# Round one of a graph-attention kernel: turns in pairs behind every second block, VectorE's edge codes one block later

## The chip, the cores and the metric

The kernel runs on one core of one Trainium2 chip. The metric is the time of one execution on the device, in microseconds. Three runs of the kernel before took 787.05 (the median), 786.87 and 788.37 us.

## The reference, cut to what matters

A layer norm, a graph attention layer over 4096 nodes with a dense 4096 x 4096 adjacency matrix, then a second layer (a state-space block). Only the attention touches the change:

```python
e = leaky_relu(feat_1 + feat_2.T, 0.2)       # rank one, before the nonlinearity
U = softmax(where(adj > 0, e, NEG_INF), axis=1)
prop_u = (0.5 * U) @ x                       # first product with U
rowsum = sum(U * (0.5 * U), axis=1)
feat = soft_threshold(f(x, prop_u, rowsum))
pu = U @ feat                                # second product with U
```

## The kernel before, in words

**The idea.** exp(leaky_relu(f1 + f2)) is exp(f1) exp(f2) where the sum is positive and exp(0.2 f1) exp(0.2 f2) where it is not. So each edge needs only one of three codes (no edge, edge with a negative sum, edge with a positive sum), and each product with U is two products with masks of ones and zeros: mask A times columns weighted one way, mask C times columns weighted the other way, scaled per row afterwards.

**Tiles and blocks.** The 4096 rows are 32 row tiles of 128. Four row tiles (`IT = 4`) are a supertile, so there are 8 supertiles. Round one is the first product with U, round two the second; round two also carries the state-space block, which is pipelined over its 32 row tiles. A row tile has 32 column tiles, taken in 4 blocks of 8 (`NB = 4`, `JB = 8`). A supertile has 16 blocks (`BLOCKS`), round one 128. Block b of a supertile works on row tile b // 4 and on column tiles 8 (b % 4) to 8 (b % 4) + 7.

**Two streams share each block of round one.** While the products of supertile G run, the codes of supertile G + 1 are made, two column tiles (`JH = 2`) for all four row tiles per block:
- SyncE loads half a megabyte of adj per block into one of four buffers (L344). The load of block h waits for the sign of block h - 4. At blocks 5, 8, 11 and 14 it also writes a row tile of the previous supertile's codes to HBM (L350), once all codes of that supertile are made; round two reads them back.
- ScalarE turns adj into bytes that say edge or no edge (`sign`, L1275).
- TensorE turns them to have columns on partitions: `turn`, four matmuls of 128 columns in bf16 with a unit matrix (L1640), into one of four PSUM banks. It waits for the sign and for the codes of four blocks back, whose bank it takes.
- VectorE compares and makes the codes (`codes`, L777), two instructions per block, which wait for the turn (`tr_done`).

**The products.** For block b ScalarE makes mask A (L1338) and VectorE mask C (L785) from the codes, two blocks ahead (`LEAD = 2`) and into one of four slots each; both wait until the product of four blocks before has ended, and for the codes. The masks of the first three blocks of a supertile need only part of the supertile's codes, those from the fourth block on need all of them (`mask1`: `NT if it else (ch + 1) * JB`, which is 32 for the fourth block as well). TensorE multiplies in two halves: 8 matmuls of 128 x 260 with mask A into accA (L1701) and 8 with mask C into accC (L1710), in float32 read in reduced form. It then turns. Before the first block of a row tile it waits until the accumulators of two row tiles ago were read (`free_acc`).

**Behind a row tile.** ScalarE reads accA in the second block of the next row tile (L1361, L1362). VectorE adds accC in the third (`sum1`, L802). GpSimd makes the tile's features out of the sum, a chain of some twenty small dependent instructions (`features`, L527 to L550). VectorE thresholds them one row tile later (`feat1`, L811 and L812), directly behind the next tile's sum.

**The order on each engine is written out by hand.** On VectorE a block of round one is: mask C for two blocks ahead, the two codes of this block, and in every fourth block a sum and a threshold. On TensorE: products, turn. On ScalarE: sign, mask A for two blocks ahead, in every fourth block a read of accA. In the last supertile there is nothing to turn; instead ScalarE (L1333), VectorE (L764) and, for three tiles, GpSimd prepare the weighted columns of round two, for which the features must be done. The line numbers in the rows are those of the kernel before.

## Time and profile before

| | |
|---|---|
| median of three runs | 787.05 us |
| the profiled execution, its own time | 786.87 us |
| its span, first to last instruction | 785.1 us |
| TensorE busy (matmuls) | 741.4 us, 94% |
| VectorE busy | 726.4 us, 93% |
| ScalarE busy | 671.1 us, 85% |
| GpSimd busy | 632.7 us, 81% |
| granted TensorE clock, mean | 0.991 of full speed |
| start of round one's steady part | 59.65 us (block 2) |
| last turn | 305.06 us |
| round two's products begin | 338.25 us |

The table gives the sums for the whole span. Engines run side by side, so the sums say nothing of which one sets the end; the order in time and the waits do. In the rows below an instruction's duration can reach over the start of the next one, because an engine takes up the next instruction before the last has drained; the step from start to start is then what one costs. Matmuls are pipelined, so theirs too are read from start to start.

### The profile page before, as it was taken

The numbers are of one execution on the slowest core, as the hardware profiler recorded it, in microseconds if no ns is written. First come the engines' busy times: TensorE is split into PE (matmuls) and PEld (weight loads), VectorE is DVE, ScalarE is ACT, GpSimd is POOL, SyncE is SP. The second block draws the span as 40 slices with busy tenths as digits, with TensorE's granted clock in tenths as the row PEclk, the third lists the DMA queues.
The fourth block names the chain that finished last, engine by engine and source line by source line (L and its number), as shares of the span: only waits on it lengthen the run. The fifth ranks groups of instructions, "written<-read, shape, count | busy, mean of one in ns | idle before, by whom it ended". The sixth has DMA issues, their size and how long they took to land.

```text
span 785.1 us, 21076 instructions
## 1 busy us (share of the span) xinstructions
PE 741.4 (94%) x6049; PEld 708.5 (90%) x6049; DVE 726.4 (93%) x1898; ACT 671.1 (85%) x1428; POOL 632.7 (81%) x1215
## 2 busy tenths in 40 slices
PE   3689999999999999987899999999999999999987
PEld 1378999999999999977899999999999999999975
DVE  6999999999999999797999999999989899989986
ACT  5999898999899898955888888888889898989865
POOL 5583788888888888886888888888888888888863
PEclk9989999999999999999999999999999999999999
DMA  7689898989898986022221212121212121210000
GB/s 218 187 258 316 288 298 272 313 276 343 260 324 283 307 286 239 18 66 68 68 65 46 68 45 68 43 67 43 67 46 67 44 69 41 70 42 18 10 4 15
DMA packets 97961, 110.43 MB, mean 141 GB/s; under 512 B 6865, under 2 KB 89713, under 8 KB 97905
## 3 DMA queue, kind: packets, MB, share of 16 engines
q1 hardware_dynamic: 97906, 109.78, 43.3%
q8 instruction: 25, 0.41, 0.2%
q14 instruction: 30, 0.25, 0.1%
HBM read 90.87 MB, written 18.89 MB: 140 GB/s over the span
## 4 chain that ended last, share of the span: by engine, by line
PE 73%; DVE 13%; POOL 7%; issue 3%; ACT 2%; DMA 1%; POOLq 0%; DVEq 0%; ACTq 0%
PE accA L1701 26%; PE accC L1710 25%; DVE code L777 4%; PE ps L1640 3%; PE ps L1808 3%; PE ps L1792 3%; PE ps L1825 2%; DVE maskC L785 2%; PE ps L1806 2%; PE ps L1790 2%; PE ps L1810 2%; PE ps L1844 2%; PE ps L1817 1%; PE ps L1827 1%; DVE Y L756 1%
## 5 line engine op out<-in xcount | busy, mean ns | idle before, releaser
L1338 ACT ACTIVATE maskA<-code 128x1024 fp32r<-128x1024 int8 x256 | 269.2, 1053 | 20.7 <-DVE code L777 17.6
L1701 PE MATMUL accA<-Y,maskA 128*128 128x260 f32 (+1 forms) x1792 | 270.0, 293 | 1.7 <-issue 1.6
L1710 PE MATMUL accC<-Y,maskC 128*128 128x260 f32 (+1 forms) x1792 | 253.2, 284 | 4.3 <-DVE maskC L785 4.3
L1701 PEld LDWEIGHTS accA<-Y,maskA 128*128 128x128 f32 x1792 | 232.3, 191 | 4.6 <-issue 2.2
L1710 PEld LDWEIGHTS accC<-Y,maskC 128*128 128x128 f32 x1792 | 228.9, 189 | 5.6 <-DVE maskC L785 5.5
L785 DVE TENSOR_SCALAR maskC<-code 128x1024 fp32r<-128x1024 int8 x256 | 206.1, 806 | 0.1
L777 DVE SCALAR_TENSOR_TENSOR code<-f_rows,neg_f,ps 128x512 int8<-128x512 int8 (+1 forms) x256 | 178.2, 739 | 1.7 <-PE ps L1640 0.5
L1275 ACT ACTIVATE edges<-adj_in 128x1024 int8<-128x1024 f32 x128 | 135.3, 1059 | 2.0 <-DMA adj_in<-in_adj_dram 2.0
L638 POOL TENSOR_TENSOR room_r<-room,room_r 128x256 fp32r<-128x256 f32 x128 | 97.7, 791 | 2.5
L1063 DVE SCALAR_TENSOR_TENSOR room<-room 128x128 f32<-128x128 f32 x270 | 86.2, 340 | 0.0
L1640 PE MATMUL ps<-ident,edges 128*128 128x128 bf16 x512 | 51.2, 224 | 10.0 <-ACT edges L1275 10.0
L1640 PEld LDWEIGHTS ps<-ident,edges 128*128 128x128 bf16 x512 | 30.1, 99 | 20.0 <-ACT edges L1275 10.8
L1701 PE MATMUL accA<-Y_2a,maskA 128*128 128x256 f32 x256 | 38.1, 291 | 0.0
L527 POOL COPY small<-roww 128x2 f32 (+1 forms) x30 | 12.4, 414 | 31.4 <-DVE ps_sum L802 30.0
L1710 PE MATMUL accC<-Y_2b,maskC 128*128 128x256 f32 x256 | 36.0, 283 | 1.5 <-DVE maskC L785 1.5
L1465 ACT COPY room<-ps 128x260 f32<-128x260 f32 x30 | 11.3, 377 | 29.8 <-PE ps L1792 29.8
L1477 ACT ACTIVATE room<-ps,room 128x128 f32<-128x128 f32 x90 | 35.2, 474 | 0.0
L1808 PE MATMUL ps<-room 128*128 128x64 f32 x248 | 34.5, 262 | 0.0
L1710 PEld LDWEIGHTS accC<-Y_2b,maskC 128*128 128x128 f32 x256 | 32.9, 192 | 1.7 <-DVE maskC L785 1.7
L1539 ACT ACTIVATE room<-room 128x64 f32<-128x64 f32 x124 | 33.3, 341 | 0.0
L989 DVE SCALAR_TENSOR_TENSOR room<-accC,roww,acc_s 128x256 f32<-128x256 f32 x32 | 15.5, 485 | 18.8 <-ACT acc_s L1359 12.9
L1808 PEld LDWEIGHTS ps<-room 128*128 128x128 f32 x248 | 32.6, 192 | 0.0
(275 smaller groups left out, 1624.0 us busy)
## 6 DMA issues: line engine op xcount, KB each, us to landing
adj_in<-in_adj_dram SPq DMA_DIRECT2D x128, 512.0 KB, 5.0
edge_codes<-code SPq DMA_DIRECT2D x32, 512.0 KB, 5.6
code<-edge_codes SPq DMA_DIRECT2D x32, 512.0 KB, 3.3
xn<-in_x_dram SPq DMA_DIRECT2D x4, 512.0 KB, 5.7
room<-in_x_dram SPq DMA_DIRECT2D x32, 64.0 KB, 1.8
room<-in_L_gnn_h_dram SPq DMA_DIRECT2D x32, 64.0 KB, 2.0
out_dram<-room SPq DMA_DIRECT2D x32, 64.0 KB, 1.6
room<-in_L_ffn_W_in_dram SPq DMA_DIRECT2D x1, 192.0 KB, 2.5
```

The costliest lines, as they stand in the source:

```text
L638: m = g.tensor_tensor(dam.rearrange("p a h w -> p (a h) w")[:, at], upto.unsqueeze(1).broadcast_to([P, NH // 2, P]), da_parts.rearrange("p ...
L777: v.scalar_tensor_tensor(out=code[par][:, :, jt * P:(jt + 1) * P], in0=f1_rows[:, rows].rearrange("p (i r) -> p i r", i=IT), scalar=neg_f2 ...
L785: v.tensor_scalar(maskC[:, b % MASKS], src, 1.0 - LINK, None, ALU.is_equal).then_inc(S["maskC_ready"], 1)
L1063: ins = v.scalar_tensor_tensor(out=conv[:, cb], in0=hist[:, kc, cb, tap:tap + P], scalar=conv_wt[:, cb, tap:tap + 1], in1=conv[:, cb], op0 ...
L1275: s.activation(pair, adj_in[:, h % 4].rearrange("p i (e w) -> p i e w", e=JH), ACT.Relu, bias=FREE, scale=HUGE).then_inc(S["signed"], 1)
L1338: s.activation(maskA[:, b % MASKS], src, ACT.Relu, bias=1.0 - LINK, scale=-1.0).then_inc(S["maskA_ready"], 1)
L1477: m = s.activation(conv[:, cb], second[:, cb * P:(cb + 1) * P], ACT.Identity, bias=conv_bt[:, cb:cb + 1], scale=conv_wt[:, cb, TAPS - 1:TAPS])
L1539: last = s.activation(xdtd[:, h * HD:(h + 1) * HD], xdt[:, h * HD:(h + 1) * HD], ACT.Copy, scale=expD[:, h, P - 1:P])
L1640: m = t_.matmul(ps[b % TRB][:, it * P:(it + 1) * P], edges[:, b % EDGE_SLOTS, it], ident2[:], start=True, stop=True)
L1701: t_.matmul(accA[k][:, 0:2 * cols], maskA[:, b % MASKS, l * P:(l + 1) * P], y2_of(jt, 0) if cols == F else Y[:, jt, 0, :, 0:cols], start=j ...
L1710: m = t_.matmul(accC[k][:, 0:2 * cols], maskC[:, b % MASKS, l * P:(l + 1) * P], y2_of(jt, 1) if cols == F else Y[:, jt, 1, :, 0:cols], sta ...
L1808: t_.matmul(ps[0][:, h * HD:(h + 1) * HD], mix_of(c)[:, h], xdt[:, h * HD:(h + 1) * HD], start=False, stop=h == (kb + 1) * P // HD - 1)
```

## The change

TensorE's turns of round one stood one behind every block. They now stand two together behind every second (odd) block: after the products of block b, b odd, come the turn of block b - 1 and that of block b. In supertile 0, whose first two blocks have no products in this loop, the first two turns stand together as before.

VectorE made the codes of block b in its loop's block b. It now makes those of block b - 1 there; the codes of a supertile's last block are made in block 0 of the next, behind that block's mask C. The waits in block 0 for mask A and for the written codes stay where they were. Nothing else is changed: the same instructions with the same operands, the same number of each.

```diff
@@ VectorE, supertile
                             dve.wait_ge(S["yA_done"], NB)
+                    if b == 0 and not first:
                         for j in range(JH):
-                            codes(G + 1, 1 - par, b * JH + j)
+                            codes(G, par, (BLOCKS - 1) * JH + j)
+                    if b > 0 and not last:
+                        for j in range(JH):
+                            codes(G + 1, 1 - par, (b - 1) * JH + j)
                     if ch == 2 and not (first and it < 1):
@@ VectorE, the last supertile
                     mask2(b + LEAD - BLOCKS, 0, b + LEAD - BLOCKS)
+                if b == 0:
+                    for j in range(JH):
+                        codes(G, 1, (BLOCKS - 1) * JH + j)
@@ TensorE, supertile
                     if first and b < LEAD:
-                        turn(G + 1, b)
+                        if b % 2:
+                            turn(G + 1, b - 1)
+                            turn(G + 1, b)
                         continue
...
                     products(G * BLOCKS + b, it % 2, b, ch, XC, 1 if first and it == 0 else None)
-                    if not last:
+                    if not last and b % 2:
+                        turn(G + 1, b - 1)
                         turn(G + 1, b)
```

## Rows read from the trace of the kernel before

**Rows 1.** The chain that ended last, shares of the span by engine.
```profile
PE 73%; DVE 13%; POOL 7%; issue 3%; ACT 2%; DMA 1%; POOLq 0%; DVEq 0%; ACTq 0%
```

**Rows 2.** Busy time by stretch: PE, PEld, DVE, ACT, POOL, clock, DMA share, GB/s.
```profile
97.00:202.00 105.00, 105.00 (x948) 102.22 (x948) 102.56 (x179) 96.43 (x118) 87.47 (x195) 1.00 0.91 295
```

**Rows 3.** TensorE in order of time (start, duration), with turns and without; its float32 loads.
```profile
203.19 0.40 PE L1640 MATMUL ps<-ident,edges 128*128 128x128 bf16 x4
203.40 1.20 PE L1701 MATMUL accA<-Y,maskA 128*128 128x260 f32 x8
204.44 1.12 PE L1710 MATMUL accC<-Y,maskC 128*128 128x260 f32 x8
205.40 0.40 PE L1640 MATMUL ps<-ident,edges 128*128 128x128 bf16 x4
...
313.01 1.12 PE L1701 MATMUL accA<-Y,maskA 128*128 128x260 f32 x8
...
314.92 1.12 PE L1701 MATMUL accA<-Y,maskA 128*128 128x260 f32 x8
...
L1701 PEld LDWEIGHTS accA<-Y,maskA 128*128 128x128 f32 x1792 | 232.3, 191 | 4.6 <-issue 2.2
```

**Rows 4.** The start of round one in order of time, TensorE and VectorE.
```profile
59.23 0.61 PE L1640 MATMUL ps<-ident,edges 128*128 128x128 bf16 x8
59.65 1.21 PE L1701 MATMUL accA<-Y,maskA 128*128 128x260 f32 x8
...
73.44 0.40 PE L1640 MATMUL ps<-ident,edges 128*128 128x128 bf16 x4
74.70 1.19 PE L1701 MATMUL accA<-Y,maskA 128*128 128x260 f32 x8 [0.86 <-issue]
...
74.12 0.48 DVE L802 SCALAR_TENSOR_TENSOR ps_sum<-accC,roww,acc_s 128x260 f32<-128x260 f32 x1
```

**Rows 5.** VectorE in order of time over two row tiles.
```profile
207.16 0.48 DVE L802 SCALAR_TENSOR_TENSOR ps_sum<-accC,roww,acc_s 128x260 f32<-128x260 f32 x1
...
208.15 0.89 DVE L785 TENSOR_SCALAR maskC<-code 128x1024 fp32r<-128x1024 int8 x1
208.96 1.39 DVE L777 SCALAR_TENSOR_TENSOR code<-f_rows,neg_f,ps 128x512 int8<-128x512 int8 x2
210.27 0.68 DVE L785 TENSOR_SCALAR maskC<-code 128x1024 fp32r<-128x1024 int8 x1
...
216.03 0.48 DVE L802 SCALAR_TENSOR_TENSOR ps_sum<-accC,roww,acc_s 128x260 f32<-128x260 f32 x1
...
224.81 0.48 DVE L802 SCALAR_TENSOR_TENSOR ps_sum<-accC,roww,acc_s 128x260 f32<-128x260 f32 x1
```

**Rows 6.** GpSimd: the first instruction of tiles 3, 24, 25, 26 and 27.
```profile
101.26 0.18 POOL L527 COPY small<-roww 128x2 f32 x1 [1.25 <-DVE ps_sum L802]
...
288.05 0.68 POOL L527 COPY small<-roww 128x2 f32 x1 [0.63 <-DVE ps_sum L802]
...
296.44 0.19 POOL L527 COPY small<-roww 128x2 f32 x1 [0.50 <-DVE ps_sum L802]
...
305.70 0.68 POOL L527 COPY small<-roww 128x2 f32 x1 [0.63 <-DVE ps_sum L802]
...
315.26 0.19 POOL L527 COPY small<-roww 128x2 f32 x1 [0.39 <-POOL row_out L550]
```

**Rows 7.** A supertile's fourth mask A on ScalarE, and the products that use it.
```profile
201.36 1.06 ACT L1338 ACTIVATE maskA<-code 128x1024 fp32r<-128x1024 int8 x1 [2.52 <-DVE code L777]
...
205.60 1.20 PE L1701 MATMUL accA<-Y,maskA 128*128 128x260 f32 x8
```

**Rows 8.** The last supertile: ScalarE's fourth mask A, and VectorE's waits for GpSimd.
```profile
307.69 1.06 ACT L1338 ACTIVATE maskA<-code 128x1024 fp32r<-128x1024 int8 x1 [2.35 <-DVE code L777]
...
324.81 0.23 DVE L811 TENSOR_SCALAR fwork<-scaled 128x128 f32<-128x128 f32 x1 [2.83 <-POOL scaled L549]
...
334.08 0.23 DVE L811 TENSOR_SCALAR fwork<-scaled 128x128 f32<-128x128 f32 x1 [2.14 <-POOL scaled L549]
```

## The prediction

> **What bounds the kernel now.** I read the chain that ended last first. Over the whole span it is TensorE for 73% [rows 1], so I asked of round one, where the edit is, whether TensorE is ever idle there. The table by stretch answers no: from 97 to 202 us it is busy for all 105.00 us, VectorE for 102.56 [rows 2]. The order in time then shows what a block costs TensorE. With a turn, block follows block every 2.21 us (203.19 to 205.40); in the last supertile, without turns, every 1.91 us (313.01 to 314.92) [rows 3]. A turn costs 0.29 us.
>
> TensorE is not alone, though. VectorE's two tiles of four blocks last 8.87 us (207.16 to 216.03) and 8.78 us (216.03 to 224.81) [rows 5], 17.65 together, and TensorE's eight blocks last 8 x 2.207 = 17.65. GpSimd's feature chain has the same period. After 305 us the chain leaves TensorE: GpSimd runs one tile behind another, VectorE waits for its result (2.83 and 2.14 us) [rows 8], and what follows is VectorE's. So I ask two things: how much TensorE gives back, and how much VectorE and GpSimd, one after the other, can take of it.
>
> **The change part by part.**
>
> *Turns in pairs.* The same 4 matmuls per block, half as many passages. Between products a turn takes 0.21 us (203.19 to 203.40), but the first half after it lasts 1.04 (203.40 to 204.44) instead of 0.96: its first matmul comes late, behind a float32 weight load that the short turn matmul before it doesn't cover [rows 3]. The pass into the turn adds about 0.01. Eight turns' matmuls that stand together now take 0.42 from the first to the next product (59.23 to 59.65) [rows 4], so a second turn adds 0.21 to 0.22. A pair costs 0.51 instead of 0.59; saving 0.075. Pairs: 7 in supertile 0 (its first two blocks stood together before), 8 in each of supertiles 1 to 6, 55 in all: 4.1 us of TensorE.
> The Trainium skill (TensorE: Matmul & The Clock Gate, The mechanism) says that a weight load overlaps running matmuls only when the row group differs. By that, all loads stand in line in any order and pairing saves 0. The trace disagrees so far: float32 loads of 191 ns [rows 3] lie under matmuls that follow each other every 0.12 us.
>
> *The waits inside the pair.* The second turn's two waits, with their register work, now stand behind four short matmuls instead of eight long ones. No row has that. The nearest is a turn followed by a product's wait, already inside the 0.21; I take 0, with 0.08 per pair (the whole saving) as the other end.
>
> *Codes one block later.* VectorE's instructions keep their kinds and number; only their order against sums and supertile ends moves. In the loop of an odd block its codes wait for the pair, in the even one they find the second turn done. A pair's light half is 2 x 1.92 = 3.84 us against TensorE's new 4.34, the heavy one 4.8 to 5.0: what the one runs late the other catches up, and masks are made over 2 us before their use, so TensorE isn't held. PSUM's four banks suffice: a turn needs the codes of four blocks back.
>
> *Start.* The sum of tile 0 has one block's codes fewer ahead of it, 1.3 us. Today it starts at 74.12, lasts 0.48, and TensorE, done turning at 73.65, starts block 8 only at 74.70 [rows 4]: 1.05 us lost, which goes. Until the sum of tile 3 TensorE gains 1.05 + 8 x 0.075 = 1.65 and VectorE 1.3 from its order and some tenths from waits that go. I take **1.7**. GpSimd's wait of 1.25 there (101.26) [rows 6] leaves it room.
>
> *Middle.* From 101.26 to 296.44 GpSimd does 22 tiles in 195.18 us [rows 6]. Its own pace: an odd tile 305.70 - 0.63 - 296.44 = 8.63, an even one 296.44 - 0.50 - 288.05 = 7.89; between tiles it needs 0.63 and 0.39 even where it waits for itself (315.26). That is 17.54 per two tiles; 11 of them 192.9 us, 2.2 less. VectorE's own pace: an odd tile 8.87 without any wait (its mask at 208.15 runs 0.81 to the next start instead of 0.60), an even one 0.99 + 4 x 1.92 = 8.67: 17.54 too. TensorE would need 17.65 - 0.30 = 17.35. So GpSimd and VectorE set the pace, and of TensorE's 3.3 us they pass on at most 2.2. The three meet with little room, so I take **1.8**.
>
> *Last supertile.* Here GpSimd's chain (tiles 26 to 29) sets the time, so 3.5 us arrive. But the last block's codes are made one block later (1.92), and ScalarE's fourth mask of the supertile waits for them (307.69) [rows 8]: it, and TensorE behind it, come only 3.5 - 1.9 = 1.6 us earlier. Cover: VectorE's waits for GpSimd of 2.83 and 2.14 us. I charge **0.1**. DMA issues stand in the same order on SyncE's queue; the spill waits for the codes 1.9 us longer, with the next loads of adj behind it, and these are held by ScalarE anyway. After 366 us nothing changes: shifted.
>
> Sum: 1.7 + 1.8 - 0.1 = **3.4 us**. The profiled execution took 786.87 us (785.1 of span, 1.8 around it), 0.18 less than the median of the runs; against the median the forecast is 783.6 us.
>
> **The rivals.**
> - *TensorE's whole gain arrives* (VectorE and GpSimd speed up once their phase moves): 1.05 + 4.1 = 5.1, 781.9. For: GpSimd's durations vary with what VectorE runs beside it. Against: both paces at 17.54. 0.06.
> - *The last supertile takes back 1.9*: ScalarE or TensorE is late for VectorE's sums after all: 1.6 gained, 785.4. For: ScalarE has no idle time from 307.69 on. Against: the waits of rows 8. 0.14.
> - *GpSimd and VectorE meet badly.* An odd tile's mask takes 0.89 us where another takes 0.68 [rows 5]; it starts within 0.2 us of GpSimd's second operation. If each tile had that, VectorE would need 2 x 8.87 = 17.74, more than today, and gain only its start, less 11 x 0.09: 0.7, 786.3. The Trainium skill (SBUF — State Buffer, Who interferes with whom) has a lock: whoever of the two starts first keeps the shared port for its whole instruction, the other blocks. The trace agrees in kind: 0.2 us more on a mask. A shift of 0.1 us in GpSimd's start can thus cost or free some tenths per tile. 0.11.
> - *Pairing saves nothing* (the waits inside, or loads in line): TensorE gains 1.05 at the start alone: 786.0. 0.08.
> - *Slower: masks A at the supertile ends.* ScalarE's mask of block 67 waits for all codes of the supertile, starts at 201.36 after 2.52 us of waiting, ends at 202.42, and TensorE takes it at 205.60 [rows 7]: 3.2 us ahead. The codes come 1.9 us later, the pair makes TensorE want it up to 0.3 earlier, and the next sign, which the next pair needs, is queued behind it on ScalarE. If VectorE also runs a microsecond behind, nothing is left; if VectorE then has to wait for the late turn, each of 7 ends costs. From 0.5 us each the gain is gone; at 0.75, 5.25 - 3.4 = 1.9 slower, 788.9. Against: such a stall only uses up TensorE's lead over VectorE. 0.07.
>
> **How the numbers follow.** Forecast 0.54, rivals 0.06, 0.14, 0.11, 0.08, 0.07. What a measurement can tell from no change is about 0.2%, 1.6 us: the bound lies at 785.5. Faster: forecast, full gain and most of the second rival, 0.70. Same: the next two and the rest, 0.23. Slower: 0.07. The range takes in the full gain below and the bad meeting above, 781.9 to 786.3, and leaves out the slower case and tails.
>
> **What would show it.** Two blocks from turn pair to turn pair in 4.34 us when nothing holds TensorE, but 4.38 on average, with short waits of TensorE at supertile ends; block 8 starting near 73.5; 17.5 to 17.6 us between every second sum; GpSimd's tile 25 starting near 292.9; VectorE waiting less for turns than now; the supertile after 305 with waits for masks A in blocks 115 to 120 that cost nothing; round two unchanged and shifted. Wrong if pairs stand 4.41 us apart (no saving), if odd masks of 0.89 us become the rule, if VectorE's long waits for GpSimd after 305 us go and the end moves less than GpSimd's tile 25, or if TensorE waits over half a microsecond for masks A at each supertile end.

## The result, and the profile after

Four runs of the changed kernel took 782.0 us in the median (781.77 to 782.38), four of the kernel before, taken with them, 787.71 us (786.87 to 789.63). The ratio is 0.9925, interval 0.9904 to 0.9945. Two later comparisons on other chips gave 0.9951 (0.9932 to 0.9970) and 0.9952 (0.9939 to 0.9966). The change is faster, by 0.5 to 0.75%; all three intervals lie below 1. On the 787.05 us of the forecast, 0.9925 is 781.2 us, just below the range; the later ratios are 783.2 us, close to the 783.6 forecast. That closeness is luck in part: the profiled one of those later executions lost 2.4 us more ahead of block 2 than the kernel before does (62.02 against 59.65 us), as the table below shows, and the forecast has no such term. The profiled execution took 781.77 us, span 780.0, against 786.87 and 785.1.

TensorE first, in order of time; it answers [rows 3]. Columns: start, duration, engine, line. L1708 is a block's half with mask A, L1717 the half with mask C, L1647 the turn.
```profile
195.80 1.20 PE L1708 MATMUL accA<-Y,maskA 128*128 128x260 f32 x8
...
199.71 0.62 PE L1647 MATMUL ps<-ident,edges 128*128 128x128 bf16 x8
200.14 1.21 PE L1708 MATMUL accA<-Y,maskA 128*128 128x260 f32 x8
...
204.05 0.40 PE L1647 MATMUL ps<-ident,edges 128*128 128x128 bf16 x4
204.64 0.40 PE L1647 MATMUL ps<-ident,edges 128*128 128x128 bf16 x4 [0.19 <-ACT edges L1282]
204.84 1.21 PE L1708 MATMUL accA<-Y,maskA 128*128 128x260 f32 x8
```
From 195.80 to 200.14 a pair of blocks takes 4.34 us: the saving of 0.07 per pair is there. At 204.05 the pair is split: the second turn waits for its sign, and block 68 starts at 204.84, 4.70 after 200.14. This is the supertile's end; ScalarE at the same place, masks at L1345 and signs at L1282, answers [rows 7]:
```profile
200.16 1.06 ACT L1345 ACTIVATE maskA<-code 128x1024 fp32r<-128x1024 int8 x1 [2.00 <-DVE code L777]
...
203.53 1.05 ACT L1282 ACTIVATE edges<-adj_in 128x1024 int8<-128x1024 f32 x1
```
The fourth mask is ready at 201.22 for the block at 202.14, 0.9 us ahead where it was 3.2, and the sign behind it ends at 204.58, which is what the second turn waited for.

VectorE, in the same order of time (L777 codes, L785 mask C, L802 sum; answers [rows 5]), first of the kernel before, a stretch not shown so far:
```profile
291.84 0.69 DVE L785 TENSOR_SCALAR maskC<-code 128x1024 fp32r<-128x1024 int8 x1
...
293.75 0.69 DVE L785 TENSOR_SCALAR maskC<-code 128x1024 fp32r<-128x1024 int8 x1
294.47 1.41 DVE L777 SCALAR_TENSOR_TENSOR code<-f_rows,neg_f,ps 128x512 int8<-128x512 int8 x2
295.79 0.48 DVE L802 SCALAR_TENSOR_TENSOR ps_sum<-accC,roww,acc_s 128x260 f32<-128x260 f32 x1
...
308.18 1.13 DVE L764 SCALAR_TENSOR_TENSOR Y<-xn,colw,Y 128x128 fp32r<-128x128 f32 x4
```
and of the kernel after, the same tile (25) and what follows in the last supertile:
```profile
290.07 0.69 DVE L785 TENSOR_SCALAR maskC<-code 128x1024 fp32r<-128x1024 int8 x1
290.67 1.40 DVE L777 SCALAR_TENSOR_TENSOR code<-f_rows,neg_f,ps 128x512 int8<-128x512 int8 x2
291.99 0.48 DVE L802 SCALAR_TENSOR_TENSOR ps_sum<-accC,roww,acc_s 128x260 f32<-128x260 f32 x1
...
303.76 0.69 DVE L785 TENSOR_SCALAR maskC<-code 128x1024 fp32r<-128x1024 int8 x1
304.37 1.40 DVE L777 SCALAR_TENSOR_TENSOR code<-f_rows,neg_f,ps 128x512 int8<-128x512 f32 x2
305.68 1.36 DVE L764 SCALAR_TENSOR_TENSOR Y<-xn,colw,Y 128x128 fp32r<-128x128 f32 x4
...
309.92 0.47 DVE L802 SCALAR_TENSOR_TENSOR ps_sum<-accC,roww,acc_s 128x260 f32<-128x260 f32 x1
...
320.47 0.21 DVE L811 TENSOR_SCALAR fwork<-scaled 128x128 f32<-128x128 f32 x1
...
329.15 0.23 DVE L811 TENSOR_SCALAR fwork<-scaled 128x128 f32<-128x128 f32 x1 [1.49 <-POOL scaled L549]
```
Before, mask to mask is 1.91 where nothing waits (291.84 to 293.75), but the codes just ahead of the sum come 0.72 after their mask instead of 0.60 (293.75 to 294.47): they waited for the turn that TensorE had only just made. The bracket is missing because the wait is short. From the sum of tile 3 to that of tile 25 there are 11 such steps in 22 tiles, each 0.10 to 0.24 us too long, 1.9 us together. After, the step is 0.60 (290.07 to 290.67): these codes belong to a turn made a block ago.

GpSimd, the kernel before, three of a tile's operations whose length depends on what VectorE does meanwhile (L535, L537, L541), tile 26:
```profile
307.66 1.17 POOL L535 TENSOR_SCALAR small<-num,small 128x1 f32<-128x1 f32 x1
308.80 1.15 POOL L537 TENSOR_TENSOR small<-small,consts 128x1 f32<-128x1 f32 x1
...
311.24 0.90 POOL L541 TENSOR_SCALAR small<-small 128x1 f32<-128x1 f32 x1
```
and after, with the starts of tiles 25 to 29 that answer [rows 6]:
```profile
292.65 0.19 POOL L527 COPY small<-roww 128x2 f32 x1 [0.39 <-DVE ps_sum L802]
...
301.89 0.68 POOL L527 COPY small<-roww 128x2 f32 x1 [0.63 <-DVE ps_sum L802]
...
303.85 0.81 POOL L535 TENSOR_SCALAR small<-num,small 128x1 f32<-128x1 f32 x1
304.62 0.56 POOL L537 TENSOR_TENSOR small<-small,consts 128x1 f32<-128x1 f32 x1
...
306.61 0.48 POOL L541 TENSOR_SCALAR small<-small 128x1 f32<-128x1 f32 x1
...
310.57 0.47 POOL L527 COPY small<-roww 128x2 f32 x1 [1.12 <-DVE ps_sum L802]
...
320.70 0.19 POOL L527 COPY small<-roww 128x2 f32 x1 [0.63 <-POOL row_out L550]
...
329.56 0.19 POOL L527 COPY small<-roww 128x2 f32 x1 [0.39 <-POOL row_out L550]
```
These three instructions take 1.85 us instead of 3.22. Before, VectorE ran mask C (from 307.57) and the weighted columns of round two (L764, from 308.18) beside the first two; now mask C stands beside L535 alone, the moved codes (304.37) beside L537, and column weights begin only at 305.68. The rest of the kernel before bears this out. In tiles 3 to 25, with codes alone beside them, L535, L537 and L541 last 0.34, 0.56 and 0.34 us; where mask C reaches over them, 0.81, 0.85 and 0.85. Not all of it arrives, though. Tile 26 is 1.6 us shorter (7.55 us instead of 9.17), but GpSimd then waits 1.12 us for the sum of tile 27 (309.92), so tile 27 starts 8.67 us behind tile 26 instead of 9.55.

ScalarE and TensorE in the last supertile, after (answers [rows 8]):
```profile
305.80 1.06 ACT L1345 ACTIVATE maskA<-code 128x1024 fp32r<-128x1024 int8 x1 [3.43 <-DVE code L777]
```
```profile
310.50 1.20 PE L1708 MATMUL accA<-Y,maskA 128*128 128x260 f32 x8 [1.17 <-ACT maskA L1345]
```
The fourth mask waits 3.43 instead of 2.35 us and TensorE then 1.17 for a later mask. The forecast foresaw this and took it as covered.

**Where the 5.1 us of span come from.** Stretches are cut at four events that every trace has: block 2 on TensorE, GpSimd's start of tiles 25 and 29, and block 144 (the seventeenth of round two).

| us | to block 2 | to tile 25 | tiles 25 to 29 | to block 144 | to the end |
|---|---|---|---|---|---|
| before | 59.65 | 236.79 | 38.05 | 51.68 | 398.9 |
| before, again | 59.59 | 236.94 | 38.05 | 51.70 | 399.7 |
| after | 59.86 | 232.79 | 36.91 | 50.85 | 399.6 |
| after, again | 62.02 | 232.73 | 36.90 | 50.85 | 399.6 |
| after, third | 60.42 | 232.62 | 36.92 | 50.90 | 399.6 |

The middle columns repeat within 0.3 us in these two kernels. The first and the last are not the change's: the start to block 2 lasted 59.0 to 63.05 us over the profiles of all versions, the last stretch 398.9 to 399.9, and versions without the later codes, described below, have the same scatter (59.4, 61.7 and 62.4 us to block 2). What the change brings in the middle is 4.00 + 1.14 + 0.83, 6.0 us; whole executions show 3.8 to 5.9 us of it. I therefore judge versions below by the stretches and give ratios beside them. A stretch has its own scatter: the version with the codes alone, profiled twice, took 721.3 and 720.2 us from block 2 to the end, so differences below 1 us between two versions are not told apart by one profile each.

### The profile page after: what moved, and what is told of

The parts are those of the page before. It is cut to its first block, busy times and chain, and to the rows that moved or that the text cites. A ratio compares the mean times of both kernels' runs of the same rounds, so it can differ in the third digit from the quotient of the medians.

```text
span 780.0 us, 21076 instructions
## 1 busy us (share of the span) xinstructions
PE 737.7 (95%) x6049; PEld 707.6 (91%) x6049; DVE 726.2 (93%) x1898; ACT 670.5 (86%) x1428; POOL 628.5 (81%) x1215
## 4 chain that ended last, share of the span: by engine, by line
PE 63%; DVE 22%; issue 6%; POOL 5%; ACT 3%; DVEq 1%; DMA 0%; ACTq 0%; POOLq 0%
PE accA L1708 21%; PE accC L1717 21%; DVE code L777 9%; DVE maskC L785 4%; PE ps L1818 3%; PE ps L1802 2%; PE ps L1835 2%; PE ps L1816 2%; PE ps L1820 2%; PE ps L1647 2%; PE ps L1854 2%; PE ps L1800 2%; PE ps L1827 1%; PE ps L1837 1%; PE ps L1843 1%
## 5 line engine op out<-in xcount | busy, mean ns | idle before, releaser
L1345 ACT ACTIVATE maskA<-code 128x1024 fp32r<-128x1024 int8 x256 | 269.2, 1054 | 20.5 <-DVE code L777 19.8
L1708 PE MATMUL accA<-Y,maskA 128*128 128x260 f32 (+1 forms) x1792 | 264.3, 290 | 1.6 <-ACT maskA L1345 1.2
L1717 PE MATMUL accC<-Y,maskC 128*128 128x260 f32 (+1 forms) x1792 | 253.4, 284 | 2.8 <-DVE maskC L785 2.7
L1708 PEld LDWEIGHTS accA<-Y,maskA 128*128 128x128 f32 x1792 | 231.5, 189 | 4.6 <-issue 2.3
L1717 PEld LDWEIGHTS accC<-Y,maskC 128*128 128x128 f32 x1792 | 229.2, 190 | 3.7 <-DVE maskC L785 3.6
L785 DVE TENSOR_SCALAR maskC<-code 128x1024 fp32r<-128x1024 int8 x256 | 206.6, 808 | 0.3
L777 DVE SCALAR_TENSOR_TENSOR code<-f_rows,neg_f,ps 128x512 int8<-128x512 int8 (+1 forms) x256 | 178.0, 738 | 0.3 <-DVE neg_f L741 0.2
L1282 ACT ACTIVATE edges<-adj_in 128x1024 int8<-128x1024 f32 x128 | 135.6, 1061 | 1.6 <-DMA adj_in<-in_adj_dram 1.6
L1647 PE MATMUL ps<-ident,edges 128*128 128x128 bf16 x512 | 42.5, 223 | 12.0 <-ACT edges L1282 11.9
L1647 PEld LDWEIGHTS ps<-ident,edges 128*128 128x128 bf16 x512 | 29.9, 99 | 20.2 <-ACT edges L1282 13.8
L1708 PE MATMUL accA<-Y_2a,maskA 128*128 128x256 f32 x256 | 38.9, 295 | 0.0
L1717 PE MATMUL accC<-Y_2b,maskC 128*128 128x256 f32 x256 | 36.1, 284 | 0.2 <-DVE maskC L785 0.2
L1717 PEld LDWEIGHTS accC<-Y_2b,maskC 128*128 128x128 f32 x256 | 33.0, 192 | 0.5 <-DVE maskC L785 0.5
L1708 PEld LDWEIGHTS accA<-Y_2a,maskA 128*128 128x128 f32 x256 | 33.3, 194 | 0.0
```

Of the source, the lines that this page charges most:

```text
L777: v.scalar_tensor_tensor(out=code[par][:, :, jt * P:(jt + 1) * P], in0=f1_rows[:, rows].rearrange("p (i r) -> p i r", i=IT), scalar=neg_f2 ...
L785: v.tensor_scalar(maskC[:, b % MASKS], src, 1.0 - LINK, None, ALU.is_equal).then_inc(S["maskC_ready"], 1)
L1282: s.activation(pair, adj_in[:, h % 4].rearrange("p i (e w) -> p i e w", e=JH), ACT.Relu, bias=FREE, scale=HUGE).then_inc(S["signed"], 1)
L1345: s.activation(maskA[:, b % MASKS], src, ACT.Relu, bias=1.0 - LINK, scale=-1.0).then_inc(S["maskA_ready"], 1)
L1647: m = t_.matmul(ps[b % TRB][:, it * P:(it + 1) * P], edges[:, b % EDGE_SLOTS, it], ident2[:], start=True, stop=True)
L1708: t_.matmul(accA[k][:, 0:2 * cols], maskA[:, b % MASKS, l * P:(l + 1) * P], y2_of(jt, 0) if cols == F else Y[:, jt, 0, :, 0:cols], start=j ...
```

## The experiments

Theory A, that of the forecast: TensorE's cheaper passages are what the middle gains, and VectorE and GpSimd pass on what they can. Theory B: the codes one block later do it, because VectorE no longer waits for a turn just made and the sum stands earlier; the pairs are only cover. Each part was made alone first.

**The codes alone.** The changed kernel with single turns, twice.
```diff
-                        if b % 2:
-                            turn(G + 1, b - 1)
-                            turn(G + 1, b)
+                        turn(G + 1, b)
...
-                    if not last and b % 2:
-                        turn(G + 1, b - 1)
+                    if not last:
                         turn(G + 1, b)
```


> Codes one block later on VectorE, turns one behind every block as before. Theory A (pairing gives TensorE 0.07 us per pair, VectorE and GpSimd set the pace, the order of the codes gives the start and the last supertile): TensorE's block stays at 2.207 us, the stall of 1.05 us before block 8 goes, GpSimd's tile 25 starts 1.0 to 1.3 us earlier, and the last supertile gives about 1 us more because VectorE's column weights come later against GpSimd's tile 26: 1.5 to 2.5 us faster in all, ratio 0.997 to 0.998. Theory B (the order of the codes brings nearly all, pairing little): 4.5 to 5.1 us faster, 0.9935 to 0.994.

> Codes alone one block later: 721.3 us from block 2 to the end in the first profile. If the pairs bring 1.2 us, it is 721.3 again, 1.2 above the changed kernel; if that was chance, the two come within 0.3 of each other. In round one up to tile 25 at most 0.3 us apart in either case.


Measured: 0.9938 (0.9926 to 0.9951) and 0.9939 (0.9925 to 0.9952), as the whole change. To tile 25: 233.1 and 231.8 us; tiles 25 to 29: 37.55 and 36.91; from block 2 to the end 721.3 and 720.2, the changed kernel 720.1 or 720.2. The second expectation said that the two would come within 0.3 us if the first difference was chance, and they did; its 0.3 us up to tile 25 were missed (231.8 against 232.6 to 232.8). TensorE keeps its turn behind every block and its 2.21 us per block:
```profile
197.12 1.20 PE L1708 MATMUL accA<-Y,maskA 128*128 128x260 f32 x8
...
199.33 1.20 PE L1708 MATMUL accA<-Y,maskA 128*128 128x260 f32 x8
```
Theory A falls for the middle: the gain is there without a cheaper passage. TensorE does come later to block 112, the first of the last supertile (243.7 and 242.7 us after block 2, the changed kernel 241.6), and it costs next to nothing, since that supertile waits for GpSimd. From the sum of tile 3 to that of tile 25, 22 tiles, it takes 193.7 and 193.5 us, the whole change 193.6, 193.9 and 193.7, the kernel before 195.2. TensorE alone would need 194.2 for them (11 x 17.65): it has a lead over VectorE and uses up some of it, so over a longer round one single turns would become the bound.

**The pairs alone.** The kernel before with its turns in pairs, VectorE's order untouched; the edit is shown against the changed kernel.
```diff
-                        for j in range(JH):
-                            codes(G, par, (BLOCKS - 1) * JH + j)
-                    if b > 0 and not last:
-                        for j in range(JH):
-                            codes(G + 1, 1 - par, (b - 1) * JH + j)
+                        for j in range(JH):
+                            codes(G + 1, 1 - par, b * JH + j)
...
-                if b == 0:
-                    for j in range(JH):
-                        codes(G, 1, (BLOCKS - 1) * JH + j)
```


> Turns in pairs, VectorE as in the kernel before: each block's codes in its own block, the sum behind them. The sum of a row tile then stands behind the codes of an even block, which wait for the turns of the odd block after it; TensorE's next row tile but one needs that sum at once, in the very next block. So TensorE waits in every fourth block for two codes and a sum, 1.3 + 0.5 us: 27 times 1.8 us less what pairing saves, 40 to 46 us slower than before. If the later codes are not needed for the pairs, the time is that of the changed kernel.


Measured: 840.95 us (one run; before 787.0), 54 us slower from block 2 on; 40 to 46 were expected. VectorE's codes of an even block wait for a turn that stands behind the next block, and the sum behind them holds TensorE's accumulators. VectorE, then TensorE:
```profile
202.01 1.41 DVE L777 SCALAR_TENSOR_TENSOR code<-f_rows,neg_f,ps 128x512 int8<-128x512 int8 x2 [2.83 <-PE ps L1640]
...
207.68 0.48 DVE L802 SCALAR_TENSOR_TENSOR ps_sum<-accC,roww,acc_s 128x260 f32<-128x260 f32 x1
```
```profile
205.92 0.62 PE L1640 MATMUL ps<-ident,edges 128*128 128x128 bf16 x8
208.39 1.22 PE L1701 MATMUL accA<-Y,maskA 128*128 128x260 f32 x8 [1.86 <-DVE ps_sum L802]
```
From 64 to 302 us VectorE waits 41.4 us for turns, 41 times, and the granted clock there is 0.96 instead of 1.00. With VectorE's order as it was, the pairs can't be had; the later codes are one order that goes with them.

**The pairs with the sum ahead of the codes**, codes in their own block; the edit is cut, against the changed kernel, whose own loops of codes are gone.
```diff
+                    if ch == 2 and not (first and it < 1):
+                        sum1(G * IT + (it - 1), (it - 1) % 2)
+                    if ch == 2 and not (first and it < 2):
+                        feat1(G * IT + (it - 2), it % 2)
+                    if not last:
+                        for j in range(JH):
+                            codes(G + 1, 1 - par, b * JH + j)
```


> Turns in pairs, each block's codes in its own block as before, but the sum and the threshold of every fourth block ahead of that block's codes instead of behind them. Theory A: the codes of an even block now wait for the pair, and what matters is only that the sum isn't behind that wait: round one runs at the same pace as in the changed kernel, its GpSimd tile 25 starts within 1 us of it, and the last supertile has the order of the kernel before, so 1 us less: 0.9945 to 0.996. Theory B: without the later codes little is gained, 0.998 or more.


Measured: 1.0021 (1.0009 to 1.0033); to tile 25 238.3 us, 1.5 more than before. Theory A's expectation missed, theory B's (0.998 or more) held. The sum no longer stands behind codes that need the pair, but VectorE comes late to it, with 0.8 us instead of 0.68 for some masks and waits of up to 0.5 us for the pair in earlier blocks, and TensorE waits for the sum in most row tiles: the sum of 201.09 ends at 201.57, TensorE's next row tile begins at 201.66. TensorE's waits from 64 to 302 us, of matmuls and of weight loads ("issue" names no releaser):
```profile
PE accA L1702 <- DVE ps_sum L802: 1.3, 6, 0.3
...
PEld accA L1702 <- issue: 5.0, 19, 0.4
```
In this version moving the sum is no substitute for moving the codes, though it takes away nearly all of the 54 us.

**The passage doubled.** In the kernel before each turn is cut in two, two of its four matmuls behind either half of a block.
```diff
+                    split = (lambda: turn_half(G + 1, b, 0)) if not last else None
+                    products(G * BLOCKS + b, it % 2, b, ch, XC, 1 if first and it == 0 else None, split)
                     if not last:
-                        turn(G + 1, b)
+                        turn_half(G + 1, b, 1)
```


> The kernel before, with each turn cut in two: two of its four matmuls between the two halves of the products, two behind them. No work more, but twice the passages between long float32 matmuls and short bf16 ones. If a passage costs TensorE 0.075 us, a block lasts 2.28 us instead of 2.21, which TensorE, VectorE and GpSimd must follow: about 8 us slower. If the passage costs nothing and it was something else that the pairs saved (the waits, the queue), the block stays at 2.21.


Measured: 792.9 us (one run; before 787.2).
```profile
200.96 1.20 PE L1711 MATMUL accA<-Y,maskA 128*128 128x260 f32 x8
...
202.10 1.20 PE L1720 MATMUL accC<-Y,maskC 128*128 128x260 f32 x8
203.14 0.28 PE L1649 MATMUL ps<-ident,edges 128*128 128x128 bf16 x2
203.24 1.20 PE L1711 MATMUL accA<-Y,maskA 128*128 128x260 f32 x8
```
A block takes 2.28 (200.96 to 203.24) instead of 2.21: 0.07 for one more passage, in the other direction. The term of the forecast is right as a price of TensorE, and once TensorE has to pay it with nothing beside it, it arrives: the 22 tiles take 200.4 instead of 195.2 us.

**Who covers the pairs?** VectorE's threshold, two instructions, is left out and one copy stands in its place; with pairs and without.
```diff
-                link(v.tensor_scalar(fwork[:, 1], scaled[:, k], -THRESH, THRESH, ALU.max, ALU.min))
-                v.tensor_tensor(mine, scaled[:, k], fwork[:, 1], ALU.subtract).then_inc(S["feat_done"], 1)
+                v.tensor_copy(mine, scaled[:, k]).then_inc(S["feat_done"], 1)
```


> The changed kernel, with VectorE's threshold of the features (two instructions per row tile, 0.59 us) replaced by one copy: the threshold of 1e-6 is left out. Theory B (VectorE sets the pace of round one, so TensorE's saving by pairs lies beside it): with about 0.35 us per row tile taken off VectorE, its own pace falls to some 16.9 us per two tiles, and now TensorE (17.4) or GpSimd (17.0 to 17.5) is the bound: from tile 3 to tile 25 about 191 us instead of 193.6, VectorE has waits again, for turns or for GpSimd. Theory A (TensorE's saving was what counted): the same as the changed kernel, 193.6.

> The same replacement in the kernel with the later codes and single turns (the threshold of 1e-6 is left out here too). Theory B: VectorE is relieved, but TensorE's two tiles still take 17.65 us and hold it, so from tile 3 to tile 25 it stays near 194 us, and the kernel with pairs and the same replacement is 2 to 3 us faster: pairing's gain appears where VectorE doesn't cover it. Theory A expects the same distance between the two as without the replacement, 1.2 us.


Measured: with pairs 0.9896 (0.9881 to 0.9911), 22 tiles in 191.0 us; with single turns 0.9921 (0.9903 to 0.9938), 194.2 us, just what TensorE needs with single turns. With VectorE relieved the pairs are worth 3.2 us over the 22 tiles, close to TensorE's 3.3 of the forecast; with the threshold in place they are worth nothing (193.6 against 193.7 and 193.5). Yet from block 2 to the end the two are only 1.0 us apart (718.3 against 719.3). The rest is gone before the 22 tiles begin: from block 2 to the sum of tile 3 the one with pairs takes 38.9 us, the other, whose block 2 came late in that profile (63.05), 36.9. One profile each doesn't say whether that is the version's or the execution's. The whole executions put 2 us between them. VectorE's waits in the first of the two, from 64 to 302 us (line, what for, total, times, longest):
```profile
DVE code L777 <- PE ps L1646: 3.8, 14, 0.4
```
VectorE now waits for TensorE; in the changed kernel that list is empty. So in the changed kernel VectorE sets the pace over these tiles.

**The supertile's last codes kept.** The last block's codes are made in that block behind those of the block before, twice.
```diff
-                    if b == 0 and not first:
-                        for j in range(JH):
-                            codes(G, par, (BLOCKS - 1) * JH + j)
...
+                        if b == BLOCKS - 1:
+                            for j in range(JH):
+                                codes(G + 1, 1 - par, b * JH + j)
...
-                if b == 0:
-                    for j in range(JH):
-                        codes(G, 1, (BLOCKS - 1) * JH + j)
```


> As the changed kernel, but the codes of a supertile's last block are made in its own last block, directly behind those of the block before, not in block 0 of the next supertile. Theory A: round one's pace is the same (17.54 us per two tiles), ScalarE's fourth mask of a supertile waits less (by 0.6 us, one mask), and in the last supertile VectorE has no codes left, its column weights start 1.3 to 1.9 us earlier against GpSimd's tile 26, which is slowed again to about 9 us: 1 us of the gain is lost, 0.9945 to 0.995. Rival C (the late codes cost time at the supertile ends through ScalarE's mask): this one is the faster, by up to 1 us against the changed kernel.

> Pairs and later codes, a supertile's last codes in its own last block: 719.7 us from block 2 to the end in the first profile. If ScalarE's late fourth mask costs the changed kernel something in the last supertile, it is 719.7 again, 0.4 below the changed kernel; if not, 720.1.


Measured: 0.9956 (0.9942 to 0.9971) and 0.9932 (0.9919 to 0.9946). The 22 tiles take 193.0 both times, 0.6 less than the changed kernel, and TensorE waits for no sign: so much do the late codes cost at the supertile ends. Tiles 25 to 29 take 36.6, to block 144 51.4 and 51.1. In all 719.7 us from block 2 to the end, both times, against 720.1, 720.1 and 720.2: 0.4 us less, as rival C and the second expectation have it, which the ratios can't tell. GpSimd's tile 26 takes 8.1 us here, 7.55 in the changed kernel, 9.17 before (first instruction to the end of L550); the first expectation had about 9 and 1 us lost by it. The trace says why 8.1: a mask C now stands beside two other operations, L539 (0.90 us, 0.43 in the changed kernel) and L549 (0.99, 0.46).
```profile
304.80 0.90 POOL L539 TENSOR_SCALAR small<-small 128x1 f32<-128x1 f32 x1
...
308.54 0.99 POOL L549 TENSOR_TENSOR scaled<-featw 128x128 f32<-128x128 f32 x1
```
And it costs nothing: here the sum of tile 27 is there in time, tile 27 starts 8.53 us behind tile 26, sooner than in the changed kernel (8.67), whose shorter tile 26 is followed by a wait. The length of tile 26 alone doesn't set this stretch.

**The same with two column weights later.**
```diff
-                for t in Y2_AT[b]:
+                for t in ([], [0, 1], [2, 3])[b] if b < 3 else Y2_AT[b]:
                     y2_low(t)
```


> The version with a supertile's last codes in its own last block (719.7 us from block 2 to the end, tile 26 on GpSimd 8.14 us), and in the last supertile VectorE's first eight column weights one block later (blocks 1 and 2 instead of 0 and 1). Theory: GpSimd's tile 26 is slowed by VectorE's column weights that run beside it, so it falls to 7.6 us and the end comes about 0.5 us earlier: 719.2 us. Rival (tile 26's length has another cause): 8.1 us again and no difference.


Measured: 0.9921 (0.9908 to 0.9935), tile 26 8.27 us, tiles 25 to 29 36.6, in all 720.3 us instead of the 719.2 expected. It missed: with the column weights gone a mask C stood beside GpSimd's chain instead (L539 lasts 1.24 us). What stands beside it matters, not only the column weights.

**Column weights back beside GpSimd.** In the changed kernel, block 0 of the last supertile, the column weights ahead of the moved codes.
```diff
                 if b == 0:
+                    for t in Y2_AT[b]:
+                        y2_low(t)
+                if b == 0:
                     for j in range(JH):
                         codes(G, 1, (BLOCKS - 1) * JH + j)
...
-                for t in Y2_AT[b]:
+                for t in Y2_AT[b] if b else []:
```


> The changed kernel, with one swap in block 0 of the last supertile: VectorE's column weights of tiles 0 and 1 stand ahead of the codes that the change has put there, not behind. If GpSimd's tile 26 is slowed by what VectorE runs beside it (masks and column weights, but not codes), its instructions L535 and L537, which took 1.13 and 1.23 us to the next start in the kernel before and 0.77 and 0.64 in the changed one, get long again and the tile takes 8.3 us or more instead of 7.55. If not, it stays at 7.55 us.


Measured: 784.66 us (one run). To tile 25 232.9 as the changed kernel, tiles 25 to 29 38.29, to block 144 51.7: 1.4 and 0.9 back, the whole gain of these stretches and a little more. The 0.9 lies behind block 136, in round two, as the 0.8 of the changed kernel does.
```profile
304.26 1.16 POOL L535 TENSOR_SCALAR small<-num,small 128x1 f32<-128x1 f32 x1
305.38 0.67 POOL L537 TENSOR_TENSOR small<-small,consts 128x1 f32<-128x1 f32 x1
...
307.31 0.84 POOL L541 TENSOR_SCALAR small<-small 128x1 f32<-128x1 f32 x1
...
311.83 0.47 POOL L527 COPY small<-roww 128x2 f32 x1 [1.65 <-DVE ps_sum L802]
```
```profile
307.24 1.06 ACT L1348 ACTIVATE maskA<-code 128x1024 fp32r<-128x1024 int8 x1 [4.52 <-DVE code L777]
```
L535 and L541 last 1.16 and 0.84 again, 2.67 for the three where the changed kernel has 1.85 and the kernel before 3.22; but L537 stays short and tile 26 takes 7.89 us, between the 7.55 and the 8.3 of the expectation, which is thus met by half. And the codes come a microsecond later, ScalarE waits 4.52 and VectorE's sum, which GpSimd waits for, is later too. It is this second thing that costs the time: GpSimd is done with tile 26 and waits 1.65 us for the sum, so tile 27 starts 9.54 us behind tile 26 because its sum stands 9.94 behind the last. What runs beside GpSimd shows in its operations, not in this version's time.

**The sum earlier.** In the changed kernel, and in the one that keeps the last codes, the sum moves ahead of the codes of its block, 1.3 us earlier.
```diff
+                    if ch == 2 and not (first and it < 1):
+                        sum1(G * IT + (it - 1), (it - 1) % 2)
                     if b == 0 and not first:
                         for j in range(JH):
                             codes(G, par, (BLOCKS - 1) * JH + j)
...
-                    if ch == 2 and not (first and it < 1):
-                        sum1(G * IT + (it - 1), (it - 1) % 2)
```


> The changed kernel, with round one's sum ahead of the codes of its block instead of behind them, the threshold still behind them. VectorE's work is the same, but GpSimd gets each sum 1.3 us earlier. If VectorE alone sets the pace up to tile 25 and GpSimd's chain from there on, GpSimd's tile 26 begins up to 1.3 us earlier, the pace before it stays at 17.6 us per two tiles, and the end comes 0.5 to 1.3 us earlier than the changed kernel's (720.1 us from block 2 to the end): 719 to 719.6. If the new phase makes GpSimd and VectorE block each other more, it is no faster or slower.

> Both together: a supertile's last codes in its own last block, and the sum ahead of the codes. From block 2 to the end 719.7 us without the early sum; with it 718.4 to 719.2 us if the reasons hold, the best of all versions, ratio to the kernel before about 0.991.


Measured: 0.9975 (0.9963 to 0.9986) and 0.9966 (0.9955 to 0.9976); 22 tiles in 196.05 and 195.8 us instead of 193.6 and 193.0, from block 2 to the end 722.8 and 721.5. Both missed, though tile 26 is at its shortest in them (7.2 and 7.1 us): GpSimd waits 2.8 us for the sum of tile 27. VectorE in the first of them, one tile:
```profile
210.25 0.90 DVE L785 TENSOR_SCALAR maskC<-code 128x1024 fp32r<-128x1024 int8 x1
211.07 1.40 DVE L777 SCALAR_TENSOR_TENSOR code<-f_rows,neg_f,ps 128x512 int8<-128x512 int8 x2
212.39 0.83 DVE L785 TENSOR_SCALAR maskC<-code 128x1024 fp32r<-128x1024 int8 x1
213.14 0.48 DVE L802 SCALAR_TENSOR_TENSOR ps_sum<-accC,roww,acc_s 128x260 f32<-128x260 f32 x1
```
Two of this tile's masks last 0.90 and 0.83 instead of 0.68, a third of the tile before too; over the 22 tiles 27 of 88 do, in the changed kernel 11. GpSimd's small operations begin at other moments of VectorE's block, and a mask loses 0.14 to 0.21 us each time. This is the rival "GpSimd and VectorE meet badly", in a version that was not asked about.

**Repeats.** The changed kernel twice more and the kernel before once more; their times stand in the table above.


> The changed kernel once more, timed beside the others and beside the kernel before, to have the size of the gain from executions that alternate. Both theories expect what its profile showed: a span 5.1 us shorter than before, so a ratio of 0.9935; if the gain is 5.9 us as the first ratio said, 0.9925. The profile should repeat the features of tile 26 on GpSimd in about 7.6 us instead of 9.2.

> The changed kernel: 720.1 us from block 2 to the end in both profiles so far, so 720.1 within 0.3 again. Whole executions: 0.993 to 0.995 of the kernel before, with starts that differ by 2 to 3 us.

> The kernel before, once more with a profile. From block 2 to the end 725.5 us as in its first profile, within 0.3; if the first profile was an odd one, the reading of all other differences shifts with it.


Measured: 0.9951, 0.9952, and 0.9997 (0.9986 to 1.0007) for before against itself. The changed kernel's stretches came as expected (720.1 us both times). The kernel before did not: 726.4 us from block 2 to the end instead of 725.5 within 0.3. Of these 0.9 us 0.8 are in the last stretch (399.7 against 398.9), which takes either value in other versions too; up to block 144 the two profiles agree within 0.2.

## Why the forecast was right and wrong

**Direction right, size too small, the cause misnamed.** Against 3.4 us forecast the stretches give 6.0, the whole executions 3.8 to 5.9.

- *Turns in pairs, 0.075 us per pair.* Right as TensorE's price: 4.34 us per pair of blocks, where two before take 4.41; doubling the passages adds 0.07 each. The idea behind it holds too: the first half after a turn lasts 1.04 (200.14 to 201.18 in the same view), the next block's 0.96 (202.14 to 203.10).
- *The waits inside the pair, 0.* Right: the second turn's waits cost nothing where the sign is there.
- *Start, 1.7.* Measured 2.4: from block 2 to the sum of tile 3 38.5 us instead of 41.0 (98.39 - 59.86 against 100.61 - 59.65). The codes alone bring it as well (38.8 and 37.6). Block 8's stall of 1.05 us is gone; it starts at 73.30, forecast near 73.5.
- *Middle, 1.8.* Measured 1.6 (195.2 to 193.6 us for 22 tiles). That is near in size by luck, and wrong in its reason. The step had VectorE's own pace right, 17.54 against 17.65 us per two tiles, but read the 0.11 between them as time that only a faster TensorE could give: "of TensorE's 3.3 us they pass on at most 2.2". Over these tiles nothing of the 3.3 was needed: with single turns, TensorE still at 17.65, VectorE takes 17.6. The gap was its 0.10 to 0.24 us in front of the last codes of every second tile, and codes of a turn made one block ago don't have it. The forecast gave that move nothing in the middle ("only their order against sums and supertile ends moves"). TensorE's saving ends in waits at the supertile ends and in a lead that the last supertile doesn't use.
- *Last supertile, minus 0.1.* **This is the step that failed in size.** It charged the late fourth mask against the cover of VectorE's waits, and the cover held: TensorE waits 1.17 us once, VectorE's wait of 2.83 us [rows 8] is gone and that of 2.14 is 1.49. But it took GpSimd's chain of tiles 26 to 29 to be as long as before, merely shifted, and never asked what the moved codes put beside it, though it had that very mechanism among its rivals, as a loss. GpSimd's tile 26 is 1.6 us shorter. Then the sum of tile 27 becomes the bound (1.12 us of waiting), so 0.9 of it arrives, and tiles 25 to 29 gain 1.1 where 0.1 was charged: 1.2 of the 2.6 us missing; the start has another 0.7, the next term 0.8. With the column weights ahead of the codes the gain is gone, by the later sum.
- *"After 366 us nothing changes: shifted".* This term, put at nothing, measured 0.8. In both kernels block 136 starts 27.5 us behind tile 29 (27.49 and 27.52), block 144 51.7 before and 50.85 after: round two itself runs differently, above all in block 136, which takes 5.65 us instead of 6.67. The change touches nothing there, and why is open.
- *The rivals.* That TensorE's whole gain arrives (781.9) came nearest in time and isn't the mechanism. The last supertile takes nothing back. GpSimd and VectorE meet well here, badly with the earlier sum. That pairing saves nothing is wrong for TensorE, near right for the whole time (0 to 1.2 us by the stretches); its 786.0 fell because it gave the codes' move nothing beyond the start. The slower case: signs late at the supertile ends by up to 0.4 us, 0.6 us in all by the version that keeps the last codes, far under the 0.5 each from which it decides.

The Trainium skill (TensorE: Matmul & The Clock Gate, The mechanism) has a weight load overlap running matmuls only when the row group differs, though the same section also lets a load into the background weight buffer go ahead of them, which the prediction left out. For this kernel the runs disagree with the first: loads of 191 ns [rows 3] lie under matmuls that follow each other every 0.12 us, and passages that differ only in their order cost 0.07 us more or less each. With the Trainium skill's lock (SBUF — State Buffer, Who interferes with whom) the runs agree in kind: masks of 0.68 us last up to 0.90 in another phase.

**Open.** What makes the 0.8 us between blocks 136 and 144: from tile 29 to block 144 the versions scatter from 50.9 to 51.7 without an order that I could find; two that have no late codes in the last supertile (the passage doubled, the early sum with the last codes kept) have 50.9 too, and the codes alone have 51.6 and 51.7. And whether the pairs bring anything at all in the whole time: the stretches say 0 to 1.2 us, the ratios nothing.

## What to carry to other kernels

When two engines run at nearly the same pace (here 17.54 and 17.65 us per two tiles), read the consumer's steps from start to start for waits too short for a bracket, and make it consume what is one block old: that was worth more here than the cheaper passages, which cost 54 us with VectorE's order untouched. A saving on one engine is worth what the next engine leaves: relieve that one in an experiment and see if the saving appears. And when instructions move, ask what they now stand beside on the other engine (here VectorE and GpSimd), for the gain as well as for the loss; then ask which wait comes next, for here only 0.9 of 1.6 us arrived.

## What the runs showed of the hardware

- GpSimd's operations on a single column change in length with what VectorE runs beside them. In tiles 3 to 25 of the kernel before, L535 lasts 0.34 us beside codes out of PSUM alone (12 times) and 0.81 where mask C reaches over it (11 times), L537 0.56 or 0.85, L541 0.34 or 0.85. In the last supertile, once each, column weights out of SBUF alone make it 0.80 for L535 and 0.49 for L541, mask C and column weights together 1.17 and 0.90.
- Moving one sum by 1.3 us, with the same instructions, cost 2.5 us over 22 tiles, and VectorE's steps behind its masks account for it: 58.0 us instead of 55.4.
- The first stretch varies by 4 us between profiles (59.0 to 63.05 to block 2), and the granted clock goes with it. From 40 to 59 us it was 0.73 in the four profiles whose block 2 started at 61.67 us or later, two of them versions with the codes in their own block (the passage doubled, the sum ahead of the codes), and 0.82 to 0.91 in the fourteen others (58.99 to 60.42). In the changed kernel's first two profiles it was 0.91, then 0.73, and block 2 started at 59.86 and 62.02. A difference of a few microseconds in the total can come from there alone.
